# Four tiny transformer layers on one core: the PSUM banks of the attention stages divided anew between the score ring and the half steps

## The reference

```python
# self attention, layers 0, 1 and 2 (layer 1 with rope; layer 2 in windows of 64 tokens)
attn_w = softmax(einsum('bhqd,bhkd->bhqk', q, k) * scale)      # 256 queries x 256 keys
x = x + gate * (einsum('bhqk,bhkd->bqhd', attn_w, v) @ W_proj + b)
# cross attention, layers 0 and 1
c_attn_w = softmax(einsum('bhqd,bhsd->bhqs', q_c, k_c) * scale)  # 256 queries x 1601 keys
x = x + einsum('bhqs,bhsd->bqhd', c_attn_w, v_c) @ W_cproj + b
# layer 2: cross attention over the 16 largest scores of each row; layer 3: a mixture of experts
```

## Time and profile before

| what | value |
|---|---|
| median of 3 runs | 4512.72 us (4508.49 to 4527.49) |
| profiled execution, its own time | 4508.28 us |
| its span | 4506.5 us |
| TensorE matmul (PE) busy | 3579.0 us, 79% |
| VectorE (DVE) busy | 3535.7 us, 78% |
| ScalarE (ACT) busy | 2958.1 us, 66% |
| GpSimd (POOL) busy | 695.1 us, 15% |
| mean granted TensorE clock | 0.807 of full speed |

### The profile page before, as it was taken

One profiled execution on the slowest core, in us unless ns is written; L12 is line 12 of the kernel. 1 busy time (PEld: TensorE's weight loads), 2 busy tenths in 40 slices (PEclk: granted clock), 3 DMA queues, 4 the chain that ended last, 5 costly groups with the idle time before them and its releaser, 6 DMA issues.

```text
span 4506.5 us, 75222 instructions
## 1 busy us (share of the span) xinstructions
PE 3579.0 (79%) x28389; PEld 1586.2 (35%) x28389; DVE 3535.7 (78%) x5424; ACT 2958.1 (66%) x5488; POOL 695.1 (15%) x1464
## 2 busy tenths in 40 slices
PE   2679999986789999878476768778787877868788
PEld 2323333332323333233132334434343443434444
DVE  7658888937668888657699999898988989899532
ACT  1455888854647888838377776767767777676652
POOL 1322121104233333013011000010100001000000
PEclk8788999997879999978566676767777777677797
DMA  4553443204433333134301111011101101000000
GB/s 137 130 116 95 102 100 91 68 27 127 111 100 95 94 86 91 32 97 115 80 27 37 36 32 38 15 41 30 38 19 32 39 20 32 23 13 13 24 14 5
DMA packets 271170, 272.96 MB, mean 61 GB/s; under 512 B 38224, under 2 KB 245592, under 8 KB 270040
## 3 DMA queue, kind: packets, MB, share of 16 engines
q1 hardware_dynamic: 270808, 268.14, 23.6%
HBM read 145.99 MB, written 120.89 MB: 59 GB/s over the span
## 4 chain that ended last, share of the span: by engine, by line
DVE 21%; PE 17%; ACT 10%; issue 3%; POOL 0%; ACTq 0%; POOLq 0%; DVEq 0%
DVE m8b L2438 6%; DVE s_sb L2435 6%; ACT un L2038 5%; DVE s_sb L2441 5%; DVE mpart L2432 4%; PE xa_ps L1912 2%; PE xa_ps L1984 2%; PE ring L1828 2%; PE xa_ps L1934 2%; ACT prob L2111 2%; PE xa_ps L1917 2%; PE ring L1858 2%; ACT s_sb L2047 1%; PE e_ps L1870 1%; PE ring L1781 1%
## 5 line engine op out<-in xcount | busy, mean ns | idle before, releaser
L1415 DVE TENSOR_REDUCE mpart<-ring 128x1 f32<-128x400 f32 (+2 forms) x2816 | 1292.7, 523 | 233.8 <-PE ring L1204 230.8
L1333 ACT ACTIVATE prob<-xa_ps 128x512 f32<-128x512 f32 (+1 forms) x2048 | 1109.8, 595 | 239.8 <-PE xa_ps L1249 218.9
L2111 ACT ACTIVATE prob<-xa_ps 128x512 f32<-128x512 f32 (+1 forms) x832 | 451.9, 597 | 307.1 <-PE xa_ps L1917 241.3
L1204 PE MATMUL ring<-k_st,q_st 52*128 52x400 bf16 (+2 forms) x2560 | 579.4, 339 | 31.0 <-DVE mpart L1415 8.5
L1781 PE MATMUL ring<-k_st,q_st 52*128 52x400 bf16 (+1 forms) x1024 | 328.9, 441 | 295.4 <-ACT s_sb L2047 275.6
L1266 PE MATMUL xa_ps<-prob,va 128*9 128x256 f32 x6656 | 507.3, 384 | 0.4 <-ACT prob L1333 0.4
L2432 DVE MAX8 mpart<-s_sb 128x8 f32<-128x1601 f32 x256 | 456.2, 1817 | 54.2 <-ACT s_sb L2047 54.2
L2047 ACT ACTIVATE s_sb<-ring 128x400 f32<-128x400 f32 (+1 forms) x1024 | 468.2, 516 | 30.8 <-PE ring L1781 22.1
L2038 ACT ACTIVATE un<-s_sb 128x1601 fp8e4<-128x1601 f32 x256 | 392.9, 1535 | 136.9 <-DVE s_sb L2441 136.7
L2435 DVE MATCH_REPLACE8 s_sb<-mpart,s_sb 128x1601 f32<-128x1601 f32 x256 | 462.0, 1813 | 0.0
L2441 DVE MATCH_REPLACE8 s_sb<-m8b,s_sb 128x1601 f32<-128x1601 f32 x256 | 461.9, 1813 | 0.0
(11 more groups left out here) (304 smaller groups left out, 4155.3 us busy)
## 6 DMA issues: line engine op xcount, KB each, us to landing
k_st<-kc_dram SPq DMA_DIRECT2D x192, 300.2 KB, 5.4
o_dram<-o_sb SPq DMA_DIRECT2D x192, 128.0 KB, 1.8
kc_dram<-k SPq DMA_DIRECT2D x72, 300.0 KB, 3.2
ctx_t<-in_ctxT SPq DMA_DIRECT2D x24, 800.5 KB, 4.7
q_st<-q_dram SPq DMA_DIRECT2D x80, 192.0 KB, 4.0
kc_dram<-k SPq DMA_DIRECT2D x72, 200.0 KB, 3.6
k_st<-k_dram SPq DMA_DIRECT2D x48, 192.0 KB, 4.9
kc_dram<-k SPq DMA_DIRECT2D x24, 300.8 KB, 3.1
```

Source lines behind the costliest of these rows:

```text
L1204: nc.tensor.matmul(ring_ps[:, r % BANKS, 0:w], q_st[rows, b % NQ, 2 * t + pl, qt * P:(qt + 1) * P], k_st[rows, slot_of(n), pl, c0:c0 + w], ...
L1333: nc.scalar.activation(prob[0:size, s % NPROB, hf * 512:(hf + 1) * 512], x_ps[0:size, (2 * s + hf) % XBANKS, :], ACT.Exp, scale=HEAD_SCALE ...
L1415: nc.vector.tensor_reduce(mpart[:, n % 4, row, c:c + 1], ring_ps[:, r % BANKS, 0:chunks[c][1]], AX.X, ALU.max).then_inc(g["red"].sem, 1)
L2111: nc.scalar.activation(prob[0:size, s % NPROB, hf * 512:(hf + 1) * 512], x_ps[0:size, (2 * s + hf) % XBANKS, :], ACT.Exp, scale=HEAD_SCALE ...
```

## The change

`BANKS` goes from 4 to 5 and `XBANKS` from 3 to 2. All eight banks become one PSUM tile, `banks`, of which the ring takes the first five, the half steps the next two and the sums the last; `Onward` still gets the first four and the last four. The wait ahead of the four matmuls of a step goes; in its place the first matmul of each half waits for the exponential that last read its bank: half 0 for a count of 2s - 1 and half 1 for a count of 2s, which is the exponential of half 1 of the step before. The wait of half 1 stands between (pl 0, half 0) and (pl 0, half 1).

```diff
--- before.py
+++ after.py
@@ -989,7 +989,7 @@
     B0 = 1 if cross else 0
     ahead = range(1, B) if cross else [0]
     q_index = lambda b: b // NQ + (1 if b % NQ >= Q_AHEAD else 0)
-    BANKS, XBANKS = 4, 3
+    BANKS, XBANKS = 5, 2
     NPROB = 5
     TAIL = 24
     if cross:
@@ -1050,10 +1050,10 @@
         table = None
         if rope:
             table = p.sb("table", [P, 2, S], F32, ctx)
-        ring_ps = p.ps("ring", [P, BANKS, 512], ctx)
-        xa_ps = p.ps("xa_ps", [P, XBANKS + 1, 512], ctx)
+        banks = p.ps("banks", [P, BANKS + XBANKS + 1, 512], ctx)
+        ring_ps, xa_ps = banks[:, 0:BANKS, :], banks[:, BANKS:, :]
         x_ps, av_ps = xa_ps[:, 0:XBANKS, :], xa_ps[:, XBANKS, :].rearrange("p (u c) -> p u c", u=2)
-        onward = None if cross else Onward(p, ctx, layer, ring_ps, xa_ps)
+        onward = None if cross else Onward(p, ctx, layer, banks[:, 0:4, :], banks[:, 4:8, :])
         block = ctx.enter_context(nc.Block())
 
         def place(i):
@@ -1241,10 +1241,10 @@
                 keys = slice(j * P, j * P + sizes[j])
                 if j == 0:
                     pe.wait_ge(g[f"mrow{n % 4}"].sem, g[f"mrow{n % 4}"].at(32 * (n // 4 + 1)))
-                if s >= 1:
-                    pe.wait_ge(g["exp"].sem, g["exp"].at(2 * s + 2 - XBANKS))
                 for pl in range(2):
                     for hf in range(2):
+                        if s >= 1 and pl == 0:
+                            pe.wait_ge(g["exp"].sem, g["exp"].at(2 * s + hf + 1 - XBANKS))
                         rows = slice(64 * hf, 64 * hf + ROWS)
                         last = nc.tensor.matmul(x_ps[0:sizes[j], (2 * s + hf) % XBANKS, pl * T:(pl + 1) * T], k_st[rows, slot_of(n), pl, keys], q_st[rows, b % NQ, 2 * t + pl, :],
                                                 start=True, stop=True)
```

## The result

The changed kernel takes **4728.79 us** (median of 3 runs, 4723.62 to 4729.91) against 4512.72: the ratio is 1.0468, with a 95% interval of 1.0429 to 1.0507. It is slower by 216 us; 4706 was forecast, in a range of 4640 to 4800. The profiled execution took 4729.91 us.

What follows compares the result with a forecast made beforehand. No engine was near its limit; waits between PE and ACT bound the kernel. A new loop of 1.54 us a step added 92 and 69 us in the cross stages and 37 in the self stages: 4508.3 + 198 = 4706, range 4640 to 4800.

Steps and rivals of the forecast that it cites:

- the three signs: Cross stages: prediction wrong if ACT runs four or more exponentials without gap, step is below 1.49 us, or clock leaves 1.00.
- nothing moves: Rival, whole kernel: time within 0.5%, 4510 us, needing a cross step of 1.39 to 1.47 us; chance 0.02.
- The mechanism: Cross steps: half 0's report stands behind the wait for half 1's previous exponential, so the 0.54 us cover is gone.
- The shortest step: Plain cross step: 0.54 + 0.595 + 0.05 + 0.36 = 1.54 us, with ends 1.49 and 1.61.
- PE's part: Loop's stretch from PE's release to the next exponential: 0.36 us, between 0.27 + 0.04 and 0.43.
- one starts every 0.54 us: End of first cross stage, before: eight exponentials in 4.32 us, taken as the 0.54 us between starts.
- Projections: Cross steps with a projection: PE is the limit, adding 0.46 us (key) or 0.67 us (value) above 1.54.
- The clock: Rival: PE idles mid-step, clock at 1.2 GHz for half of 832 steps, +330 us on top, 5040 us; chance 0.06.
- The sum: Whole kernel: first cross stage +92 us (668), second +69 (681), self stages +37, together 198 us.
- self stages: Three self stages: one bare 0.46 us gap in each of 27 units, +37 us in all; ends +10 and +78.
- The fifth bank: Ring waits, 64.7 us in 500: removed by the bank, but hidden by the new loop anyway; costed at nothing.
- The rivals for no change and for faster: No change: 4510 us, chance 0.02. Faster: fifth bank pays, new wait never last, -129 us, 4380, chance 0.02.

## Why the prediction was right, point by point

**The total and the signs.** 4729 lies in the range, 23 us above the forecast, and the direction came by the mechanism that was named. That the sum came so close is in part luck: terms were wrong both ways. Of the three signs by which the prediction called itself wrong, two came: the plain step is 1.465, below 1.49, and the clock of the cross stages is 0.95, not 1.00. The third, four exponentials in a row without a gap, did not come: no two steps of the cross stages start less than 1.45 us apart. The rival "nothing moves" had named a step of 1.39 to 1.47 us as its condition. The plain step does lie there, and the kernel is 4.7% slower all the same: 1.385 was the mean with the projections in it, and the mean after is 1.64 (681.9/415), so that condition couldn't tell the two apart.

**The mechanism.** Half 0 is reported behind a wait for the exponential right ahead of it on ACT, and the 0.54 us of cover are gone: shown. The wait with the later count makes it (three half banks, same form, no loss), and its price follows the ring's terms (1.46 and 1.57 us).

**The shortest step** was forecast at 1.54, with 1.49 as its low end; it is 1.465. Two terms were too large. PE's part was 0.36 and is 0.32, almost the low end. And "one starts every 0.54 us" was wrong. Looked at one by one, the exponentials at the end of the first cross stage of before start at 941.57, 942.06 (a pair of 1.08 whose second lasts 0.59) and 942.65; the last row is PE:

```profile
941.57 0.60 ACT L1333 ACTIVATE prob<-xa_ps 128x512 f32<-128x512 f32 x1
...
941.57 1.08 ACT L1333 ACTIVATE prob<-xa_ps 128x512 f32<-128x512 f32 x2
...
942.65 1.08 ACT L1333 ACTIVATE prob<-xa_ps 128x512 f32<-128x512 f32 x2
942.22 0.39 PE L1249 MATMUL xa_ps<-q_st,k_st 55*128 55x256 bf16 x4
```

Within a step they are 0.49 apart, between steps 0.59: there the next one starts only when the last has ended, so ACT did wait, by some 0.1. The step of 1.08 before was a loop as well: 0.60 to the end of half 0's exponential, 0.05 to PE at 942.22, and 0.43 to the next exponential of half 0 at 942.65. I divided a merged row by its count, and took a mean of two intervals for ACT's own pace. The Trainium skill, "ScalarE: Activation LUTs", section "What ACT_TABLE_LOAD costs", says that back-to-back activations overlap by about 93 ns; 0.595 - 0.50 in the pairs agrees, and the 0.055 that I had read between them could have warned me. Over 416 steps the error is 31 us for each stage, too high.

**Projections** were forecast to add 0.46 and 0.67 us. A key projection of the first cross stage, PE with its weight load, then ACT:

```profile
525.46 0.11 PEld L1249 LDWEIGHTS banks<-q_st,k_st 55*128 55x128 bf16 x3 [0.33 <-ACT prob L1333]
525.78 0.94 PE L1218 MATMUL banks<-ctx_t,w 128*128 128x401 f32 x2
...
527.48 0.45 PE L1249 MATMUL banks<-q_st,k_st 55*128 55x256 bf16 x3
525.79 1.09 ACT L1333 ACTIVATE prob<-banks 128x512 f32<-128x512 f32 x2 [0.38 <-PE banks L1249]
...
527.98 1.08 ACT L1333 ACTIVATE prob<-banks 128x512 f32<-128x512 f32 x2 [0.62 <-PE banks L1249]
```

The step is 527.98 - 525.79 = 2.19 us, 0.73 above 1.465; one with a full value projection is 413.29 - 410.89 = 2.40, 0.94 above. Adding PE's own work failed at its ends, not in its size. From the second matmul of one step's scores (525.46) to the first of the next (527.48) PE takes 2.02 us, and 2.00 was forecast. But the exponential follows the former by 0.33 us and the latter, where all four matmuls are still to come, by 0.50: 2.02 + 0.50 - 0.33 = 2.19. The kernel before, with 0.42 and 0.49 us at the two ends, took 2.09 for most such steps. Counted over the whole first cross stage, the 28 steps with a key projection average 2.35 us and the 21 with a full value projection 2.49: 25 + 22 = 46 us above 1.465, in place of 27.

**The clock** was a rival with 0.06, taken as all or nothing. It came in small: some 17 us in each cross stage, and not in the plain steps, for which the stage's end spoke rightly, but where a unit's values are missing and then doubled. I had counted the eight matmuls of a self unit and missed that a cross unit has the same place. The comparison with the stage's end was weaker than I put it: it set 1.12 us of work beside 0.89, but of steps of 1.54 and 1.08, so PE was to be busy for 0.73 of the new step, and had been for 0.83 of the old one. The rule of the Trainium skill, "TensorE: Matmul & The Clock Gate", section "A second HAM failure mode: psum-queue depth-cycling", which I had set aside, is borne out in part: the clock does go up and down here, at a tenth of the price of the rival, but the waits at PSUM banks don't suffice. The version without a step that lacks its values has the same loop of waits and a clock of 0.98 in the first cross stage.

**The sum.** First cross stage +107.6 from first to last line 1249 (forecast +92), second +88.2 (+69), self stages +7.4, +5.5 and +7.8 (+37 in all). The errors went both ways. For the first cross stage, counted step by step in the trace, against the forecast of 668: shorter steps -31, projections +19, value projections of a single tile, costed at nothing, +3, steps with doubled values +22 (the clock is most of that), other steps +3. That is 684; measured are 681.9. In proportion the self stages are the term that was most off, by nearly half. One trace is a weak measure of them: the second takes 126.0 us in the kernel before, and 128.3 to 131.4 in the three versions with three half banks that are as fast. A self unit is 191.63 - 188.28 = 3.35 us, 0.37 above 2.98:

```profile
188.28 1.08 ACT L1333 ACTIVATE prob<-banks 128x512 f32<-128x512 f32 x2 [0.38 <-PE banks L1249]
...
190.16 1.08 ACT L1333 ACTIVATE prob<-banks 128x512 f32<-128x512 f32 x2
191.63 1.08 ACT L1333 ACTIVATE prob<-banks 128x512 f32<-128x512 f32 x2 [0.38 <-PE banks L1249]
```

One gap of 0.38 is bare and the other covered by sums and maxima, as forecast; but with 27 such units a stage would get 10 us longer, and it got 5 to 8 longer. That waits for the maxima took up the rest is likely, as the low end of the forecast had it, but was not read unit by unit.

**The fifth bank** was costed at nothing, since the new loop would hide the ring's waits in any case. It did: they fell to 20.4 us without the fifth bank and to 13.1 with it. Its worth is some 21 us at the measured ratios, not told apart from nothing. The rivals for no change and for faster are out.

## What to carry to other kernels

Before a buffer is taken from one ring for another, write down for each report which wait stands ahead of it in the stream, and follow the ring of waits around: a report behind a wait for the consumer's latest work turns overlap into a sum. The price of such a wait is the ring's terms and what is queued behind it. Take an engine's pace from single instructions, not from a merged row.

## What the runs showed that I had not expected

One step in thirteen without its values was enough for the granted clock to fall to its 1.2 GHz level, once PE waited in the others too. The same step exists in the kernel before, where the cross stages kept 0.99, and in the version with two half banks and half 1 behind two ring items, whose first cross stage kept 0.99 too. So two half banks alone don't bring the fall; what in the waits before that step decides was not settled.

The place of half 1 in the stream costs 2.0% with three half banks, where no wait was thought to be late. No prediction here had that term.
